# A mixture-of-experts kernel's compaction: one comparison of places and a block mask in place of sixteen comparisons of slots

## The reference

```python
B, S, D = x.shape; E = Wr.shape[1]; N = B * S              # N = 2048 tokens, E = 8 experts
k = max(MIN_CAPACITY, ceil(N * CAPACITY_FACTOR / E))       # k = 512 slots for each expert
xt = x.reshape(N, D)
scores = softmax(xt @ Wr, axis=-1)
G, idx = top_k(scores.T, k)                                # for each expert its 512 best tokens
X_in = xt[idx]
h = gelu(einsum('ekd,edh->ekh', X_in, W1) + b1[:, None, :])
X_e = einsum('ekh,ehd->ekd', h, W2) + b2[:, None, :]
contrib = (G[..., None] * X_e).reshape(E * k, D)
out = zeros((N, D)).at[idx.reshape(-1)].add(contrib)       # and then x + out
```

## Time and profile before

| | us |
|---|---|
| median of 3 runs | 1232.92 |
| lowest, highest of them | 1227.31, 1253.6 |
| span of the profiled execution | 1237.5 |
| busy in it: TensorE, Vector, ScalarE, GpSimd | 1004.8, 785.4, 634.3, 465.5 |

### The profile page before, as it was taken

How to read it: one execution, slowest core, us unless ns; L and a number is a source line. 1 busy time by engine, 2 the same in 40 slices (tenths; PEclk the granted TensorE clock), 3 DMA queues, 4 the chain that set the end, 5 groups by cost and what they waited for, 6 DMA issues and landing times. The chain is left out here.

```text
span 1237.5 us, 23101 instructions
## 1 busy us (share of the span) xinstructions
PE 1004.8 (81%) x7273; PEld 814.9 (66%) x7273; DVE 785.4 (63%) x2242; ACT 634.3 (51%) x1275; POOL 465.5 (38%) x657
## 2 busy tenths in 40 slices
PE   4897899889889897998889988878623588888895
PEld 3675677667667676777667766657422477777784
DVE  4675686757586576667647857427046588787763
ACT  3574577656756855775575784346210234343441
POOL 3413233333152352334315223123130366666672
PEclk9998689977987987997888898677765699898998
DMA  5800230230023023004102202200030044444331
GB/s 190 279 2 10 69 103 1 64 117 9 0 85 102 0 85 95 8 10 139 39 0 85 77 1 87 68 1 18 1 119 34 19 101 103 102 102 102 99 72 17
DMA packets 70972, 80.89 MB, mean 65 GB/s; under 512 B 3312, under 2 KB 67184, under 8 KB 70896
## 3 DMA queue, kind: packets, MB, share of 16 engines
q1 hardware_dynamic: 64752, 71.63, 17.9%
q0 software_dynamic: 6144, 8.39, 4.2%
HBM read 71.62 MB, written 8.39 MB: 65 GB/s over the span
## 5 line engine op out<-in xcount | busy, mean ns | idle before, releaser
L725 ACT ACTIVATE probs<-neg,neg_max 128x256 f32<-128x256 f32 x512 | 232.3, 505 | 62.5 <-DVE neg_max L588 62.1
L596 DVE TENSOR_TENSOR p_lo<-ps_t,p_hi 128x512 f16<-128x512 f32 x256 | 176.5, 689 | 120.1 <-ACT p_hi L733 118.4
L733 ACT ACTIVATE p_hi<-ps_t 128x512 f16<-128x512 f32 x256 | 150.8, 589 | 131.6 <-PE ps_t L372 131.3
L372 PE MATMUL ps_t<-ident,probs 128*128 128x128 f32 x1024 | 198.7, 325 | 6.1 <-ACT probs L725 5.3
L372 PEld LDWEIGHTS ps_t<-ident,probs 128*128 128x128 f32 x1024 | 127.5, 161 | 46.9 <-issue 11.5
L588 DVE CUSTOM_DVE_ANT_0 neg<-ps_s,bias_t 128x256 f32<-128x256 f32 x256 | 97.7, 420 | 62.6 <-issue 32.6
L921 POOL TENSOR_TENSOR o_sum<-o_raw 128x128 f32<-128x128 f32 x64 | 30.0, 469 | 273.1 <-ACT o_raw L817 273.1
L588 DVE CUSTOM_DVE_ANT_0 neg<-ps_s,mask_add 128x256 f32<-128x256 f32 x224 | 85.5, 420 | 62.6 <-issue 41.6
L343 PE MATMUL ps_m<-part_h,select 32*128 32x256 f32 x256 | 77.5, 363 | 48.0 <-DVE part_l L602 22.6
L343 PEld LDWEIGHTS ps_m<-part_h,select 32*128 32x128 f32 x256 | 48.6, 211 | 64.7 <-issue 38.1
L1375 PE MATMUL ps_o<-w_h,hid_h 128*128 128x256 f32 x256 | 78.3, 306 | 13.0 <-DVE hid_l L1314 12.6
(11 more groups left out here) (239 smaller groups left out, 2460.6 us busy)
## 6 DMA issues: line engine op xcount, KB each, us to landing
bias_t<-in_bias SPq DMA_DIRECT2D x16, 2048.0 KB, 8.5
w1e<-in_w1e SPq DMA_DIRECT2D x8, 1024.0 KB, 4.9
w2e<-in_w2e SPq DMA_DIRECT2D x8, 1024.0 KB, 5.5
ctxT_A<-in_ctxT SPq DMA_DIRECT2D x8, 256.0 KB, 8.4
mask_int<-in_mask SPq DMA_DIRECT2D x8, 256.0 KB, 7.8
v_raw_A<-in_ctx SPq DMA_DIRECT2D x8, 256.0 KB, 7.9
w<-in_w SPq DMA_DIRECT2D x2, 1024.0 KB, 8.8
ctxT_C<-in_ctxT SPq DMA_DIRECT2D x8, 256.0 KB, 2.7
```

The source lines that it names most:

```text
L372: ins = nc.tensor.matmul(ps_t[u % 2][:, (i * QT + kb) * P:(i * QT + kb + 1) * P], probs[:, u % 2, i, kb * P:(kb + 1) * P], ident[:, :], st ...
L596: nc.vector.tensor_tensor(p_lo[:, u % 4, :], ps_t[u % 2][:, :], p_hi[:, u % 4, :], ALU.subtract).then_inc(lo_ready, 1)
L725: ins = nc.scalar.activation(probs[:, u % 2, i, :], neg[:, u % 4, i, :], ACT.Exp, bias=neg_max[:, u % 4, i:i + 1], scale=-1.0)
L733: nc.scalar.activation(p_hi[:, u % 4, :], ps_t[u % 2][:, :], ACT.Copy).then_inc(hi_ready, 1)
```

## The change

A slot number is taken apart into its block (slot / 128, from 0 to 3) and its place in the block (slot mod 128). `ve_slots` now does this once for all experts: it compares each slot with 0, 128, 256, 384 and 512 (`slot_ge`), takes neighbours' differences (`in_block`, 1 in the one block that the slot is in, nowhere for -1), adds up three of the comparisons (`block_no`), and subtracts 128 times that (`place`). For each expert, `ve_onehot` multiplies `info` with `in_block`, which gives 4 x 5 columns with the token's information in the columns of its block and zeros in the others (`block_info`), and makes one comparison of 16 x 128 elements (`onehot`, 128 tokens x 128 places for each tile). `pe_compact` then needs one matmul for each tile, with 20 columns. A tensor_tensor with broadcast operands takes the place of tensor_scalar instructions with one scalar for each partition.

```diff
-            nc.vector.tensor_scalar(slot[:, :, :], slot_1[:, :, :], -1.0, None, ALU.add).then_inc(S["slots_ready"], 1)
+            step(nc.vector.tensor_scalar(slot[:, :, :], slot_1[:, :, :], -1.0, None, ALU.add))
+            firsts = moe_f32[:, 3 * P:3 * P + ST + 1].rearrange("p (o s) -> p o s", o=1)
+            step(nc.vector.tensor_tensor(slot_ge[:, :, :, :].rearrange("p t e s -> p (t e) s"),
+                                         slot[:, :, :].rearrange("p t (e o) -> p (t e) o", o=1)
+                                         .to_broadcast([P, NTILE * E, ST + 1]),
+                                         firsts.to_broadcast([P, NTILE * E, ST + 1]), ALU.is_ge))
+            nc.vector.tensor_tensor(in_block[:, :, :, :].rearrange("p t e s -> p (t e) s"),
+                                    slot_ge[:, :, :, 0:ST].rearrange("p t e s -> p (t e) s"),
+                                    slot_ge[:, :, :, 1:].rearrange("p t e s -> p (t e) s"), ALU.subtract)
+            step(nc.vector.tensor_reduce(tok(block_no), slot_ge[:, :, :, 1:ST].rearrange("p t e s -> p (t e) s"),
+                                         AX_X, ALU.add))
+            nc.vector.scalar_tensor_tensor(tok(place), tok(block_no), -float(P), tok(slot), ALU.mult, ALU.add
+                                           ).then_inc(S["slots_ready"], 1)
...
             wait(ve, S["comp_out"], e)
-            for t in range(NTILE):
-                ins = nc.vector.tensor_scalar(onehot[:, t, :], iota[:, :], slot[:, t, bass.ds(e, 1)], None, ALU.is_equal)
-            ins.then_inc(S["onehot_ready"], 1)
+            nc.vector.tensor_tensor(block_info[:, :, :, :],
+                                    in_block[:, :, bass.ds(e, 1), :].rearrange("p t o s -> p t (o s)")
+                                    .rearrange("p t (s o) -> p t s o", o=1).to_broadcast([P, NTILE, ST, 5]),
+                                    info[:, :, bass.ds(e, 1), :].to_broadcast([P, NTILE, ST, 5]), ALU.mult)
+            nc.vector.tensor_tensor(onehot[:, :, :], place[:, :, bass.ds(e, 1)].to_broadcast([P, NTILE, P]),
+                                    moe_f32[:, 2 * P:3 * P].rearrange("p (o s) -> p o s", o=1).to_broadcast([P, NTILE, P]),
+                                    ALU.is_equal).then_inc(S["onehot_ready"], 1)
...
-            for st in range(ST):
-                for t in range(NTILE):
-                    ins = nc.tensor.matmul(ps_c[:, st * 8:st * 8 + 5], onehot[:, t, st * P:(st + 1) * P],
-                                           info[:, t, bass.ds(e, 1), :].rearrange("p o c -> p (o c)"),
-                                           start=(t == 0), stop=(t == NTILE - 1))
+            for t in range(NTILE):
+                ins = nc.tensor.matmul(ps_c[:, 0:ST * 5], onehot[:, t, :],
+                                       block_info[:, t, :, :].rearrange("p s c -> p (s c)"),
+                                       start=(t == 0), stop=(t == NTILE - 1))
```

More of the change, by code:

```diff
@@ L119, in build @@
         bits = sb("bits", [P, ROUNDS, CANDS * E], I32)
-        moe_f32 = sb("moe_f32", [P, 2 * P + CAP + NTILE + 1])
-        comp = sb("comp", [P, ST, 8])
+        moe_f32 = sb("moe_f32", [P, 3 * P + ST + 1 + NTILE + 1])
+        comp = sb("comp", [P, ST, 5])
         idx = [sb(f"idx{i}", [P, ST], U32) for i in range(2)]
@@ L211, in build @@
         info = sb("info", [P, NTILE, E, 5], BF16)
-        iota = sb("iota", [P, CAP], FP16)
-        onehot = sb("onehot", [P, NTILE, CAP], BF16)
+        slot_ge = sb("slot_ge", [P, NTILE, E, ST + 1])
+        in_block = sb("in_block", [P, NTILE, E, ST])
+        block_no = sb("block_no", [P, NTILE, E])
+        place = sb("place", [P, NTILE, E])
+        onehot = sb("onehot", [P, NTILE, P], BF16)
+        block_info = sb("block_info", [P, NTILE, ST, 5], BF16)
         xg = sb("xg", [P, ST, D])
@@ L1166, in ve_route @@
             nc.vector.tensor_copy(upper_b[:, :], moe_f32[:, P:2 * P])
-            nc.vector.tensor_copy(iota[:, :], moe_f32[:, 2 * P:2 * P + CAP])
-            tiles = moe_f32[:, 2 * P + CAP:2 * P + CAP + NTILE].rearrange("p (t o) -> p t o", o=1)
+            tiles = moe_f32[:, 3 * P + ST + 1:3 * P + ST + 1 + NTILE].rearrange("p (t o) -> p t o", o=1)
             nc.vector.tensor_copy(info[:, :, :, 0], tiles.to_broadcast([P, NTILE, E]))
-            part = moe_f32[:, 2 * P + CAP + NTILE:].rearrange("p (t o) -> p t o", o=1)
+            part = moe_f32[:, 3 * P + ST + 1 + NTILE:].rearrange("p (t o) -> p t o", o=1)
             nc.vector.tensor_copy(info[:, :, :, 1], part.to_broadcast([P, NTILE, E]))
@@ L1276, in ve_onehot @@
             wait(ve, S["comp_out"], e)
-            for t in range(NTILE):
-                ins = nc.vector.tensor_scalar(onehot[:, t, :], iota[:, :], slot[:, t, bass.ds(e, 1)], None, ALU.is_equal)
-            ins.then_inc(S["onehot_ready"], 1)
+            nc.vector.tensor_tensor(block_info[:, :, :, :],
[5 more added lines that the diff above has]
+                                    ALU.is_equal).then_inc(S["onehot_ready"], 1)
         def ve_slot_tokens(ve, e, par):
             ve.wait_ge(S["comp_out"], e + 1)
-            nc.vector.tensor_copy(comp[:, :, :], ps_c[:, 0:ST * 8].rearrange("p (s c) -> p s c", c=8)
+            nc.vector.tensor_copy(comp[:, :, :], ps_c[:, 0:ST * 5].rearrange("p (s c) -> p s c", c=5)
                                   ).then_inc(S["comp_copied"], 1)
@@ L1645 @@
         "moe_f32": np.concatenate([np.ones((P, P)), np.triu(np.ones((P, P)), 1),
-                                   np.broadcast_to(np.arange(CAP), (P, CAP)),
+                                   np.broadcast_to(np.arange(P), (P, P)), np.broadcast_to(np.arange(ST + 1) * P, (P, ST + 1)),
                                    np.broadcast_to(np.arange(NTILE), (P, NTILE)), part[:, None]], 1).astype(np.float32),
```

## The result

The changed kernel is not faster but a little slower. Its median is 1248.95 us (1234.33 to 1263.09, 16 runs) against 1239.73 us (1227.31 to 1253.6, 16 runs) for the kernel before on the same chips; the ratio is 1.008, 95% interval 1.005 to 1.011. The ratio leaves out each kernel's runs that are more than 1.5% above its fastest, so it isn't quite that of the medians. The forecast was 16 us less.

The account below looks back on a forecast made before the run. It took the expert stage to be bound by the onehot stall behind GpSimd's subtractions. Terms -16.7 (experts 0 to 5), +0.5 (expert 6) and -0.2 (start) gave -16.4 us, from 1232.9 to 1216 us; range 1211 to 1222, with rivals 1206 to 1235.

Parts of the forecast that it names:

- What bounds it: Expert stage: one onehot comparison stalls 5.62 us behind GpSimd's w1_l subtractions, delaying y_e; without it y_e waits for TensorE.
- The step that failed: Experts 0 to 5: block_info and the long comparison, 2.7 us together, cost nothing, covered by TensorE's matmuls and the gather.
- the second rival: The long comparison holds up the gather, xg lands 2.2 us later, cycle 31.6 us, total 1230 us; chance 0.10.
- The rival's own price: Gather held: cycle 31.6 us, experts 0 to 5 gain only 3.5 us, 0.3 given back, total 1230 us; chance 0.10.
- The start: Once ahead of the experts: four ve_slots instructions add 2.4 us, first onehot saves 1.6, first compaction 1.0; sum -0.2 us.
- The second `ve_onehot` runs under the first gather: Ahead of the experts: the second expert's comparison is hidden by the first gather, with no cost counted in the sum.
- The cycle without the stall: Experts 0 to 5 fall from 32.19 to 29.4 us each, 16.7 us less; expert 6 takes 0.5 us more.
- The matmuls: Compaction on TensorE: 1.2 us less in each of seven experts, costed at nothing; bounds 0 and 8.4 us.
- The clock: Rival: 48 matmuls behind the gather run at TensorE's low clock, cycle 34.5 us, total 1252 us; chance 0.07.
- Behind all four subtractions: Rival: the comparison waits for all four w1_l subtractions, ending at idx + 13.6 us; total 1234 to 1235 us; chance 0.10.
- my reading of the flags: Threshold's flags: a pair takes 1.16 us alone, 2.24 beside GpSimd, so a two-operand instruction loses one subtraction, 1.08 us.

Follow-up runs that it names:

- four pieces: Changed kernel with its 2048-element comparison cut into four tensor_tensor instructions of 512 elements; ratio to the kernel before 0.985, cycle 30.5 us, stage 312.3 us.
- moved: Changed kernel with both new per-expert instructions, unchanged, put behind the first y_e in Vector's order; ratio to the kernel before 0.993, cycle 30.3 us, stage 312.4 us.
- the last version: Changed kernel with only the comparison put behind xT_l and two extra TensorE matmuls in four w2 steps; ratio to before 0.990, stage 306.6 us.
- 64-matmul run: The four pieces kernel with the compaction's sixteen matmuls issued four times over; one run, cycle 30.3 us, stage 311.7 us.
- the same kernel at the old addresses: Changed kernel with unused space behind moe_f32, so the layers' tiles lie where the kernel before has them; ratio to before 1.000, stage 324.7 us.
- two-input run: The moved kernel plus an unneeded 2048-element tensor_tensor with two SBUF inputs at the old place; one run, cycle 31.7 us, stage 320.9 us.

## Why the prediction was wrong

- *What bounds it* was right: the `onehot` stall behind `w1_l` went as forecast, and `y_e` then waited for TensorE.
- *The step that failed* is "So I cost both new instructions at nothing in experts 0 to 5. Their cover is TensorE's second row of matmuls and the gather." The cover was real for Vector, but the gather isn't only cover: it is issued by GpSimd in just those 2.3 us. The comparison delays the fourth issue by 2.05 us in six experts, 12.3 us, on the chain, of the 19.5 us by which the stage missed (16.4 less forecast, 3.1 more measured). I had this as the second rival (0.10) and gave it up too cheaply: "sixteen comparisons in the same place didn't visibly stretch them" compares instructions of 0.35 us and one full SBUF input with one of 2.28 us and two. The second input is what holds the issue at all (0.96 us beside a one-input instruction of the same 2.28 us), and the length says for how long: 0.44 us more with four pieces, 2.04 with one.
- *The rival's own price* was right in the cycle, 31.6 us: expert 1 took 1043.75 - 1012.21 = 31.54, and experts 3 and 5 the same within 0.05. What it left out, by the trace of after, is three things. Experts 2 and 4 take 0.8 us more than that; ScalarE loads a table at their start (below), and their `idx` comes 0.7 us later. Before, the same two were only 0.4 us longer than their neighbours. Expert 0 takes 1012.21 - 977.64 = 34.6 us: its transposes and 48 matmuls ran at the low clock, 1.97 + 7.53 us instead of 1.10 + 5.75, 2.7 us, and its `idx` comes 0.3 us later than expert 1's. The third is the start.
- *The start* was forecast at -0.2 us. The instructions were sized right (2.38 us for 2.4, comparison and `block_info` 2.7, compaction 0.6). "The second `ve_onehot` runs under the first gather" failed in the same way: from the finished slots to expert 0's first matmul it was 975.86 - 956.86 = 19.0 us and is 977.64 - 957.35 = 20.3, so 1.3 more. The first gather's issue alone, 3.03 us instead of 1.24, is 1.8.
- *The cycle without the stall*, 29.4 us, was 0.9 to 1.1 us too short even with the hold gone (moved, four pieces), 0.6 in the last version. `idx` at the start + 14.41 was 1026.78 - 1012.21 = 14.57, in even experts 15.3; and TensorE's 27 matmuls took 5.3 us. I took expert 6's clock of 1.00 for granted.
- *The matmuls* at nothing: right up to `idx`, by the 64-matmul run; by the clock they are worth 0.2 us a cycle the other way.
- *The clock* as a rival: the low clock was there (a granted clock of 0.58 over 6.5 us, below), and its sign too, 0.89 over most experts against the 0.95 that I had named. But only in expert 0 did it fall on the 48 matmuls, where I had put it; in experts 1 to 5 it was over before the gathered rows had landed.

The stretch of expert 1, and of its second w2 block alone (columns as in the earlier trace rows):

```profile
1012.20:1043.70 31.50, 28.44 (x170) 24.61 (x169) 19.87 (x26) 12.28 (x22) 23.00 (x16) 0.89 0.30 82
...
1030.40:1036.90 6.50, 5.91 (x28) 5.67 (x28) 3.03 (x4) 0.00 (x0) 5.87 (x5) 0.58 0.21 63
```

ScalarE's table load at the start of expert 2:

```profile
1045.45 1.28 ACT L1423 ACT_TABLE_LOAD   x1
```

- *Behind all four subtractions* didn't happen in the changed kernel, because the comparison ends before they begin. But my reading of the flags, that a two-input instruction loses one subtraction and not four, doesn't hold in general: beside `w1_l`, `block_info` lost all that were left, up to 5.27 us.
- *The total.* By the trace the changed kernel is 3.1 us slower from the routing on: experts 0 to 5 together 0.8, expert 6 0.75 (0.5 forecast), the start 1.3, expert 7 and what follows it 0.7, less 0.4 ahead of the finished slots. The timed ratio says 10 us, 6 to 14; the same kernel at the old addresses says 0 us, -5 to +5. What lies between isn't settled: the three layers vary by 26 us between profiles, and no run here tells a small constant part in them from that.

## What to carry to other kernels

When a long Vector instruction takes the place of many short ones, look at what GpSimd issues in that window: here an instruction with two SBUF inputs held the issue of an indirect DMA until its end, so its length, and not Vector's total, is what the gather paid. Place such an instruction where GpSimd neither gathers nor is waited for, or cut it into pieces. And when two things change at once, as length and number of inputs did here, ask for each by itself before you call a rival unlikely. When a stall is removed, work out the chain behind it with TensorE's clock and ScalarE's table loads in it, since the stall had hidden them as well.

## What the runs showed of the hardware that wasn't expected

- An indirect DMA's issue on GpSimd takes 0.95 us alone, 0.96 us beside a 2.28 us Vector instruction with one SBUF input, and 2.6 to 3.0 us beside one with two. It ends 0.83 us after the Vector instruction that held it in the changed kernel, the two-input run and the four pieces alike, and later two-input pieces don't hold it again.
- A tensor_scalar of 128 bfloat16 elements (0.25 us alone) waits for four subtractions that follow each other without a gap, 5.7 us. A tensor_tensor with two SBUF inputs (0.48 us alone) does so as well, 5.27 us, while one of the threshold's flags got in after one subtraction. What decides this isn't shown.
- TensorE's granted clock fell to the lower level in every cycle of the four-piece version (0.87 to 0.89 over each of experts 0 to 6), behind steps with three matmuls in 1.07 us. With five in each of the last four steps it stayed at 1.00 in two experts of seven and was 0.89 to 0.94 in the others. With 48 matmuls more in the compaction it was 0.94 in experts 1 to 5.
